# Attention: the last query tile's probabilities are turned by a DMA exchange through DRAM and by block transposes on VectorE

## The reference

```
q = x @ Wq + bq;  k, v = split(x @ Wkv + bkv)        # 16 heads of 64
q, k = rope(q), rope(k)
scores = einsum('bqhd,bkhd->bhqk', q, k) / 8, masked to the causal triangle
probs  = softmax(scores)
out    = einsum('bhqk,bkhd->bqhd', probs, v) @ Wo + bo
```

## Time and profile before

| | us |
|---|---|
| runs of the kernel before | 2680.13 median (2679.9 to 2682.92, 3 runs) |
| the profiled execution's own time | 2676.49 |
| its span, first to last instruction | 2674.6 |
| PE busy in the span | 2483.8 (93%), granted clock 0.975 |
| DVE / ACT / POOL busy | 1771.4 / 1531.2 / 1448.2 |
| transposes of probabilities on PE (L1678, x2560) | 389.0 |
| copies of turned blocks, ACT (L1563, x384) / DVE (L1461, x256) | 228.0 / 175.1 |
| maximum on DVE (L1447, x512) | 410.2 |
| time to landing of an `att_zs` swap DMA, 128 KB | 2.3 |

### The profile page before, as it was taken

How to read it: one execution, slowest core, us unless ns; L and a number is a source line. 1 busy time by engine, 2 the same in 40 slices (tenths; PEclk the granted TensorE clock), 3 DMA queues, 4 the chain that set the end, 5 groups by cost and what they waited for, 6 DMA issues and landing times. The chain is left out here.

```text
span 2674.6 us, 52748 instructions
## 1 busy us (share of the span) xinstructions
PE 2483.8 (93%) x16856; PEld 1872.2 (70%) x16856; DVE 1771.4 (66%) x3259; ACT 1531.2 (57%) x3861; POOL 1448.2 (54%) x1268
## 2 busy tenths in 40 slices
PE   7986899799999999899999999999999987986999
PEld 5752677577777777677777776777777765752676
DVE  6741478477777777677777776777777765741476
ACT  2421444477777777677777776777777752421343
POOL 1100444577677677676776776767767741100342
PEclk9998999899999999999999999999999998997999
DMA  7459553323233232232332323323323226459453
GB/s 247 149 211 410 198 170 119 81 70 86 70 77 85 69 77 73 74 86 70 77 85 69 77 71 76 85 70 77 85 69 78 70 57 229 141 210 413 164 159 99
DMA packets 244597, 326.61 MB, mean 122 GB/s; under 512 B 52960, under 2 KB 197984, under 8 KB 240224
## 3 DMA queue, kind: packets, MB, share of 16 engines
q1 hardware_dynamic: 244320, 323.21, 39.5%
HBM read 211.98 MB, written 44.04 MB: 96 GB/s over the span
## 5 line engine op out<-in xcount | busy, mean ns | idle before, releaser
L1548 ACT ACTIVATE att_prob<-att_ps_s,att_nmax 128x384 f32<-128x384 f32 (+3 forms) x1024 | 528.5, 528 | 338.0 <-DVE att_nmax L1447 328.2
L1350 POOL TENSOR_TENSOR att_z_sb<-att_z_sb,att_cos 128x512 f32<-128x512 f32 x255 | 328.4, 1288 | 413.0 <-DMA att_zs<-att_z_sb 413.0
L1447 DVE TENSOR_REDUCE att_nmax<-att_ps_s 128x2 f32<-128x768 f32 (+3 forms) x512 | 410.2, 822 | 13.2
L1678 PE MATMUL att_ps_p<-sh_ident,att_prob 128*128 128x128 f32 x2560 | 389.0, 276 | 25.8 <-ACT att_probT L1563 13.9
L1353 POOL TENSOR_TENSOR att_z_sb<-att_z_sb,att_zs 128x512 f32<-128x512 f32 x255 | 351.5, 1379 | 20.0
L1678 PEld LDWEIGHTS att_ps_p<-sh_ident,att_prob 128*128 128x128 f32 x2560 | 293.2, 140 | 64.4 <-ACT att_probT L1563 17.7
L1351 POOL TENSOR_TENSOR att_zs<-att_zs,att_sin 128x512 f32<-128x512 f32 x255 | 329.1, 1290 | 0.0
L1689 PE MATMUL att_ps_p<-att_probT,att_v_sb 128*64 128x512 f32 (+3 forms) x2048 | 307.0, 442 | 1.5 <-ACT att_probT L1563 1.5
L1563 ACT COPY att_probT<-att_ps_p 128x512 f32<-128x512 f32 x384 | 228.0, 599 | 105.8 <-PE att_ps_p L1678 105.8
L1689 PEld LDWEIGHTS att_ps_p<-att_probT,att_v_sb 128*64 128x64 f32 x2048 | 136.6, 137 | 188.5 <-issue 168.2
L1444 DVE TENSOR_TENSOR att_ps_s<-att_ps_s,att_masked 128x256 f32<-128x256 f32 (+1 forms) x384 | 195.7, 510 | 65.0 <-PE att_ps_s L1664 63.4
(11 more groups left out here) (199 smaller groups left out, 5564.3 us busy)
## 6 DMA issues: line engine op xcount, KB each, us to landing
att_zs<-att_z_sb SPq DMA_DIRECT2D x512, 128.0 KB, 2.3
ffn_w<-in_e_W SPq DMA_DIRECT2D x56, 1024.0 KB, 13.7
att_R<-inverse_sums SPq DMA_DIRECT2D x256, 128.0 KB, 3.3
...
```

What stands on the lines that cost most here:

```text
L1350: nc.gpsimd.tensor_tensor(z[:, m, i, :], z[:, m, i, :], cos[:], ALU.mult)
L1447: nc.vector.tensor_reduce(nmax[:, p % 2, qt, :], ps[:, :, at:at + (qt + 1) * P], AX.X, ALU.max, negate=True)\
L1548: nc.scalar.activation(prob[:, p % 2, hh, PLACE[qt]], ps[:, hh, at:at + (qt + 1) * P], ACT.Exp, bias=nmax[:, p % 2, qt, hh:hh + 1], accum_ ...
L1678: last = nc.tensor.transpose(turn_bank(k)[:, at:at + P], prob[:, p % 2, hh, PLACE[qt]][:, kb * P:(kb + 1) * P], g.ident[:])
```

## The change

Only the blocks of query tile 3 (`LAST`) change their way: eight of the 20 blocks of a pair. `exps` writes them into a new tile `last`, arranged by groups of 32 keys. SP's new `put` stores that tile to DRAM (512 KB in one DMA), and its new `get` loads it back in four DMAs of 128 KB, each for 32 partitions, so that the block of 32x32 elements with keys b*32.. lands on the partitions b*32... DVE's new `turn` transposes the 32x32 blocks of 128x1024 elements in one instruction into `lastT`, in the place of its copy of group 3. PE keeps 12 blocks in three groups, of which ACT copies two and DVE one. `mix` runs key blocks 0 to 2 on query tiles 0 to 2 (widths 384, 256, 128) and then four products of width 128 for each head on `lastT`. In SP's order `put` comes after `rows`, `spread` goes ahead of `swap`, and `get` follows `swap`. Wo is staged in `prob` instead of `probT`. `Setup` counts on two semaphores where it had seven.

```diff
+    QUERIES_MM, MATRIX_MM, TURN_MM = 1, 2, 3
+    QUERIES, BLOCKS, MATRIX, TURNED = DC, 2 * DC, 2 * DC + 2, 2 * DC + 3
...
-        self.q_mm, self.q_done, self.blk_done, self.g_mm, self.g_done, self.zeroed, self.t_mm, self.t_done = (
-            sem(f"setup_{n}") for n in ("q_mm", "q_done", "blk_done", "g_mm", "g_done", "zeroed", "t_mm", "t_done"))
+        self.mm, self.made, self.zeroed = (sem(f"setup_{n}") for n in ("mm", "made", "zeroed"))
...
-    WIDTH = [S - kb * P for kb in range(TT)]
+    LAST, QB = TT - 1, P // QUAD
+    WIDTH = [LAST * P - kb * P for kb in range(LAST)]
     OFF = {}
-    TURNS = (None, ((0, 1), (0, 3)), ((0, 2), (1, 2)), ((1, 1), (1, 3)), ((0, 0),), ((1, 0),))
+    TURNS = (None, ((0, 0), (0, 2)), ((1, 0), (1, 2)), ((0, 1), (1, 1)))
     at = 0
...
-    pt_mm, pta_s, ptv_s, pv_mm = c("pt_mm", 5 * NP), c("pta", 3 * NP), c("ptv", 2 * NP), c("pv_mm", NP)
+    pt_mm, pta_s, ptv_s, pv_mm = c("pt_mm", 3 * NP), c("pta", 2 * NP), c("ptv", NP), c("pv_mm", NP)
+    put_s, got_s, turn_s = c("put", 16 * NP), c("got", 64 * NP), c("turn", NP)
...
-    PLACE = [slice(o, o + (qt + 1) * P) for qt, o in enumerate((0, 128, 384, 768))]
+    PLACE = [slice(o, o + (qt + 1) * P) for qt, o in enumerate((0, 128, 384))]
...
-        prob = sb("prob", [P, 2, 2, FULL])
+        prob, last = sb("prob", [P, 2, 2, FULL]), sb("last", [P, 2, QB, 2, TT, QUAD])
+        got, lastT = sb("got", [P, QB, 2 * TT, QUAD]), sb("lastT", [P, 2 * TT, P])
...
-        raw_wo = probT[:, 0:2048].rearrange("p (c n) -> p c n", c=PAIRS)
+        raw_wo = prob[:].rearrange("p m h n -> p (m h n)")[:, 0:2048].rearrange("p (c n) -> p c n", c=PAIRS)
...
+            def put(j, u):
+                need_held(sp, exp_s, j, 8 * u + 4)
+                need_held(sp, got_s, j, 64 * (u - 1))
+                sp.dma_start(last_dram[u % 2], last[:, u % 2].rearrange("p b h k c -> p (b h k c)")).then_inc(put_s.sem, 16)
+
+            def get(j, u):
+                need_held(sp, put_s, j, 16 * (u + 1))
+                need_held(sp, turn_s, j, u)
+                blocks = last_dram[u % 2].rearrange("(t r) (k n) -> k r t n", r=QUAD, k=QB)
+                for kb in range(QB):
+                    sp.dma_start(got[kb * QUAD:(kb + 1) * QUAD].rearrange("r t a c -> r t (a c)"), blocks[kb]).then_inc(got_s.sem, 16)
+
...
             def slot(t):
                 j, p = t.j, t.p
                 if t.has(p - 1):
                     rows(j, p - 1)
+                if t.has(p):
+                    put(j, p)
                 if p == XRES:
                     need_held(sp, xo_s, j, 2 - NP)
                     sp.dma_start(xres[:], tiles(x_dram, j)).then_inc(xres_in.sem, 16)
                 if p == X_LOAD and not t.last:
                     need_held(sp, xt_mm, j, DC)
                     sp.dma_start(xin[:], tiles(x_dram, j + 1)).then_inc(x_in.sem, 16)
+                if t.has(p - 1):
+                    spread(j, p - 1)
                 if t.has(p + 2):
                     swap(j, p + 2)
-                if t.has(p - 1):
-                    spread(j, p - 1)
+                if t.has(p):
+                    get(j, p)
...
             def copy_pt(j, p, k):
                 need(dve, pv_mm, j, p)
-                dve.wait_ge(pt_mm.sem, pt_mm.at(j, 5 * p + k))
+                dve.wait_ge(pt_mm.sem, pt_mm.at(j, 3 * p + k))
                 a = OFF[TURNS[k][0]]
                 nc.vector.tensor_copy(probT[:, a:a + S], turn_bank(k)[:]).then_inc(ptv_s.sem, 1)
+
+            def turn(j, p):
+                dve.wait_ge(got_s.sem, got_s.at(j, 64 * (p + 1)))
+                need(dve, pv_mm, j, p)
+                nc.vector.transpose(lastT[:].rearrange("p a (t r) -> p t a r", r=QUAD), got[:]).then_inc(turn_s.sem, 1)
             def divide(j, p):
...
                 if t.has(p - 1):
-                    copy_pt(j, p - 1, 3)
+                    turn(j, p - 1)
...
                 i = (2, 2, 0, 1)[qt]
                 ps, at = ps_s[(3 * p + i) % 2], dict(UNITS[i])[qt]
-                need(act, pt_mm, j, 5 * (p - 1))
+                if qt == LAST:
+                    need(act, put_s, j, 16 * (p - 1))
+                else:
+                    need(act, pt_mm, j, 3 * (p - 1))
                 need(act, inv_s, j, 2 * (p - 1))
                 act.wait_ge(max_s.sem, max_s.at(j, 4 * p + (1, 2, 4)[i]))
                 for hh in range(2):
-                    nc.scalar.activation(prob[:, p % 2, hh, PLACE[qt]], ps[:, hh, at:at + (qt + 1) * P], ACT.Exp,
+                    dst, src = prob[:, p % 2, hh, PLACE[qt]] if qt < LAST else None, ps[:, hh, at:at + (qt + 1) * P]
+                    if qt == LAST:
+                        dst = last[:, p % 2, :, hh].rearrange("p b k c -> p k b c")
+                        src = src.rearrange("p (k b c) -> p k b c", b=QB, c=QUAD)
+                    nc.scalar.activation(dst, src, ACT.Exp,
                                          bias=nmax[:, p % 2, qt, hh:hh + 1],
                                          accum_out=sums[:, p % 2, hh, qt:qt + 1]).then_inc(exp_s.sem, 1)
...
                 if t.has(p - 1):
-                    copy_pt(j, p - 1, 4)
-                    copy_pt(j, p - 1, 5)
+                    copy_pt(j, p - 1, 3)
...
             def transposes(j, p, k):
                 if k == 2:
                     need(pe, on_s, j, p)
-                elif k == 4:
-                    pe.wait_ge(pta_s.sem, pta_s.at(j, 3 * p + 1))
-                elif k in (3, 5):
-                    pe.wait_ge(ptv_s.sem, ptv_s.at(j, 2 * p + (k - 1) // 2))
+                elif k == 3:
+                    pe.wait_ge(ptv_s.sem, ptv_s.at(j, p + 1))
                 at = 0
                 for hh, kb in TURNS[k]:
-                    for qt in range(kb, TT):
+                    for qt in range(kb, LAST):
                         last = nc.tensor.transpose(turn_bank(k)[:, at:at + P], prob[:, p % 2, hh, PLACE[qt]][:, kb * P:(kb + 1) * P], g.ident[:])
                         at += P
                 last.then_inc(pt_mm.sem, 1)
             def mix(j, p):
-                pe.wait_ge(pta_s.sem, pta_s.at(j, 3 * p + 3))
-                pe.wait_ge(ptv_s.sem, ptv_s.at(j, 2 * p + 2))
+                pe.wait_ge(pta_s.sem, pta_s.at(j, 2 * p + 2))
+                pe.wait_ge(ptv_s.sem, ptv_s.at(j, p + 1))
+                pe.wait_ge(turn_s.sem, turn_s.at(j, p + 1))
                 pe.wait_ge(v_s.sem, v_s.at(j, 2 * (p // 2) + 2))
+                values_of = lambda kb, hh: v[:, (p // 2) % 2, kb, (p % 2) * P + hh * ADH:(p % 2) * P + (hh + 1) * ADH]
+                for kb in range(LAST):
+                    for hh in range(2):
+                        nc.tensor.matmul(mix_bank[of_head(hh), kb * P:LAST * P], values_of(kb, hh), probT[:, OFF[hh, kb]:OFF[hh, kb] + WIDTH[kb]],
+                                         start=(kb == 0), stop=(kb == LAST - 1))
                 for kb in range(TT):
                     for hh in range(2):
-                        col = (p % 2) * P + hh * ADH
-                        last = nc.tensor.matmul(mix_bank[of_head(hh), kb * P:S], v[:, (p // 2) % 2, kb, col:col + ADH],
-                                                probT[:, OFF[hh, kb]:OFF[hh, kb] + WIDTH[kb]], start=(kb == 0), stop=(kb == TT - 1))
+                        last = nc.tensor.matmul(mix_bank[of_head(hh), LAST * P:S], values_of(kb, hh), lastT[:, hh * TT + kb, :],
+                                                start=(kb == 0), stop=(kb == TT - 1))
                 last.then_inc(pv_mm.sem, 1)
...
                 for u in first_value:
                     values(t, u, 1)
-                if turned:
-                    transposes(j, p - 1, 3)
                 for u in t.values()[1:]:
                     for half in range(2):
                         values(t, u, half)
                 if out:
                     output(t, p - OUT0, 0)
                 if turned:
-                    transposes(j, p - 1, 4)
+                    transposes(j, p - 1, 3)
                 if out:
                     output(t, p - OUT0, 1)
-                if turned:
-                    transposes(j, p - 1, 5)
...
+        last = nc.dram_tensor("last_tile_blocks", (2, P, 2 * S), F32, kind="Internal").ap()
...
```

38 lines of the change are left out of this document (19 added, 19 removed).

## The result

| | kernel before | changed kernel | forecast |
|---|---|---|---|
| median, us (runs of this comparison) | 2679.9 (2677.44 to 2682.92, 5 runs) | 2664.8 (2657.43 to 2666.54, 5 runs) | 2605 (2582 to 2685) |
| ratio, with its 95% interval | | 0.994 (0.9923 to 0.9956) | 0.972 |
| span of the profiled execution | 2674.6 | 2662.0 | |
| PE busy | 2483.8 | 2383.0 | |

The changed kernel is faster by 15 us where 75 were forecast. The direction was right; the size was missed by a factor of five. The time lies inside the stated range only because that range reaches up to rival (b)'s time and beyond; it is outside the forecast's own 2590 to 2630.

What follows compares the result with a forecast made beforehand. PE's work was taken to bound plain slots at 12.77 us, afterwards DVE's ring at 11.88. 2676.49 - 85 + 10 = 2601.5 us for the profiled execution, plus 3.6 for the median: 2605, range 2582 to 2685, its own range 2590 to 2630.

Steps and rivals of the forecast that it cites:

- rival (b): Swaps land late behind `put` or `get`, making POOL late; 0.4 us a slot, about 2655 us in all; chance 0.15.
- transpose of 128x1024: DVE's block transpose replacing its copy of group 3: 1.24 us, and 1.16 to the next instruction's start.
- PE's own plain slot: PE's work alone in a slot other than 5 and 6, without turn groups 3 and 5: 12.77 - 0.95 = 11.82 us.
- `mix` in 28 instructions: PE's `mix` keeps its columns in 28 instructions instead of 16: no added time taken, at most 1.3 us.
- ring of a plain slot: Scores unit 2 through ACT, `query_low`, copy, transpose, `result` and mask to the next unit 2: 11.88 us, setting the slot.
- unit 2 of slot 4 to slot 5: Same ring with the statistics' 2.21 us added: 14.09 us where 13.53 stood, a loss of 0.56.
- unit 2 of slot 5 to slot 6: Step in which the next image's x is turned: two fewer turn groups give about 0.4 us; 15.2 us.
- lateness of the swap and POOL: POOL delayed by swaps landing later under the new traffic: 0.6 us an image, +10 us in all.
- an image: Sum over one image's slots: six steps of -0.89, then +0.56 and -0.41, together -5.2 us, giving 100.4 us.
- rival (a): DVE's transpose is stretched or slow, at 2.4 us; plain slots lose 0.25 us, some 2730 us in all; chance 0.12.
- the step on DMA, SP and POOL: DMA share about 0.67 is no bound; `put`, `spread`, `swap` and `get` fit; only POOL's lateness costs, +10 us.
- the prediction's own sign of being wrong: The forecast is wrong if POOL's query sum is what ACT waits for; no size given.

Runs made afterwards that it cites:

- experiment 4: Changed kernel with the swap DMAs issued ahead of the spread and DVE's transpose placed ahead of `query_low`; 2582.26 us, ratio 0.9658 to the kernel before.
- experiment 1: Changed kernel with the swap DMAs issued ahead of the spread DMAs, `get` still last; 2627.92 us, ratio 0.981 to the kernel before.
- experiment 2: Changed kernel without `put` and `get`, `turn` reading the tile of exponentials directly, tile 3's output not the reference's; 2613.18 us, ratio 0.9751.
- Experiment 11: experiment 1 with the query projection ahead of scores unit 2 in slot 5 alone; 2606.57 us, ratio 0.9718 to the kernel before.
- experiment 5: Changed kernel with `spread` issued ahead of `put`; 2770.9 us, ratio 1.0334 to the kernel before.
- experiments 9 and 10: 9: changed kernel with `put` behind `swap`, directly ahead of `get`, 2708.07 us; 10: experiment 4 with `put` behind `swap` and `spread`, 2709.63 us.
- experiment 3: Changed kernel with DVE's transpose placed ahead of `query_low`; 2630.43 us, ratio 0.9812 to the kernel before.

## Why the prediction was right and wrong, step by step

| step | forecast | measured |
|---|---|---|
| transpose of 128x1024 | 1.24, 1.16 to the next start | 1.234, 1.16 |
| PE's own plain slot | 11.82 | 11.73 (experiment 4) |
| `mix` in 28 instructions | no more | 1.42 to 3.74 of the slot, 2.3 as before |
| ring of a plain slot | 11.88 | 11.89 (experiment 1, slot 0) |
| unit 2 of slot 4 to slot 5 | 14.09 | 14.19; 13.70 where nothing is stretched |
| unit 2 of slot 5 to slot 6 | 15.2 | 16.71; 15.49 without a fall of the clock (experiment 2) |
| lateness of the swap and POOL | 0.6 us an image | about 3 us an image (experiment 2 against the changed kernel) |
| an image | 100.4 | 105.68 |

**What held.** The price of the transpose, which decided rival (a), was right to 0.01 us: nothing stretched it. The Trainium skill, "SBUF — State Buffer", section "SBUF: two separate sides", ties the lock on the shared port pair to two SBUF inputs, and this case's trace agrees on both sides: the transpose with one input keeps 1.234 in the mean of 128, and `query_low` with two takes 1.10 beside POOL's `key_low` instead of 0.69. The transpose was put to that test: 28 of the 128 ran beside an instruction of POOL for over 0.6 us, the longest taking 1.240, and 105 of 128 in experiment 4, the longest 1.236. The path that sets the time in a plain slot is the forecast's ring, and in slot 5 PE stood idle behind the exponentials, mostly for 1.9 to 2.3 us where 2.4 were said.

**What failed: the step on DMA, SP and POOL.** The prediction held that `spread` and `swap` both fit behind `put`, and took 0.6 us an image, 10 us in all, for lateness "since the last swap piece is issued 4 us after `put`". Rival (b) named the mechanism with 0.4 us a slot and a chance of 0.15, and it is the one that came; so did the prediction's own sign of being wrong, that ACT waits for POOL's query sum (39 slots). Its times of issue were right: `put` leaves 5.2 us after the mask and the swap 7.5 (forecast 5 and 7.5). It did not follow what lies between: `put`'s wait holds the 256 KB of `spread` back until just before the swap, and the swap's packets queue behind them.

What it cost is read best from scores unit 2 to scores unit 2, because the slot's start moves against it. Means over images 1 to 14 without 5 and 10:

| kernel | 0 to 1 | 1 to 2 | 2 to 3 | 3 to 4 | 4 to 5 | 5 to 6 | 6 to 7 | 7 to 0 | sum |
|---|---|---|---|---|---|---|---|---|---|
| forecast | 11.88 | 11.88 | 11.88 | 11.88 | 14.09 | 15.2 | 11.88 | 11.88 | 100.6 |
| after | 11.97 | 13.09 | 12.81 | 12.25 | 14.19 | 16.71 | 11.89 | 12.58 | 105.5 |
| experiment 2, no exchange | 11.91 | 12.10 | 12.13 | 12.13 | 13.70 | 16.65 | 11.89 | 11.89 | 102.4 |

Of the 4.9 us that an image is above the forecast:

- The exchange and its order in the queue: 105.5 - 102.4 = 3.1 us, of which 2.5 lie in the six plain steps. This is the term that the prediction had at 0.6.
- `query_low` beside `key_low`: also without the exchange the six plain steps are 0.8 us above the forecast, nearly all in the three from slot 1 to slot 4. There `query_low` takes 0.79, 0.90 and 0.92 us in the mean instead of 0.69, 0.5 us together, and in the other slots 0.69 throughout. It is an old collision in part, since before the change it took 0.87 and 0.83 in slots 2 and 3, where PE's own work hid it. The forecast had counted POOL's 0.89 us against its slack toward ACT only, and kept `query_low` at 0.69 in the sum.
- The clock in slot 5: 8 falls of 1.55 us in these 12 images, 1.0 us an image. The prediction named an idle time of 2.4 us and priced it as idle time alone. Experiment 11 removed the falls by filling the idle time.
- The step from slot 5 to slot 6 without a fall is 15.49 and not 15.2: of the 0.4 us that two turn groups less should give, 0.14 came. In the other direction the statistics were 0.4 us shorter than forecast. These terms add up to 4.8. Not explained is why two of the changed kernel's four images without a fall took 16.45 and 16.69 in this step.

The wrong forms of the explanation fell too. "The spread must be early" failed in experiment 5 and "put must be late" in experiments 9 and 10. What stands after them: SP's queue has a chain of waits (exponentials for `put`, `put`'s landing for `get`, the landing of `rows` for `spread`), and of the five orders that were run the best is the one of experiment 1, with `put` early, the swap next, and `spread` and `get` behind. It keeps waits and data away from the swap, but not from the x load, which still stands directly behind `put`; an order with `put` early and x ahead of it was not run.

Experiments 1 and 3 brought 37 and 34 us and both together 83 by the medians; by the ratios 35, 34 and 76, each uncertain by some 5 us, so that the excess over the sum is not clear of noise. The waits speak for it: two rings of almost equal length, DVE's with the transpose and POOL's with the swap, where taking either away alone leaves the slot to the other (ACT's waits for POOL rose to 52.2 us in experiment 3). That the two images with the loop's turn gained 1.2 and 4.3 us was not looked into.
